# Preparing the shared weights of a mixed shared and expert layer: 5 tiles ahead and 23 in the first group

## The reference

```
x = x + (einsum('bsd,bdh->bsh', x, W[cat_ids]) + b[cat_ids][:, None, :])
h = gelu(einsum('bnd,hd->bnh', x, fc1_w) + fc1_b, approximate=False)      # 2048 hidden
shared   = einsum('bnh,sh->bns', h, fc2_w) + fc2_b                        # 384 columns
expert_x = einsum('bnh,bph->bnp', h, experts_w[indices]) + be[:, None, :] # 128 columns
x = x + concatenate([shared, expert_x], axis=-1)
```

## Time and profile before

| | |
|---|---|
| timed runs | 1692.08 us (1691.57 to 1693.65, n = 3) |
| profiled execution | 1690.38 us, of it span 1688.6 us |
| TensorE matmul | 1662.6 us busy, 98% of the span, 7297 instructions |
| VectorE | 1155.4 us, 68% |
| ScalarE | 549.1 us, 33% |
| GpSimd | 210.7 us, 12% |
| 16 DMA engines | 56.5% of their span for SyncE's queue (211.35 MB), 0.1% for ScalarE's (0.79 MB) |
| granted TensorE clock | 0.995 over the span |

### The profile page before, as it was taken

One profiled execution on the slowest core, in us unless ns is written; L12 is line 12 of the kernel. 1 busy time (PEld: TensorE's weight loads), 2 busy tenths in 40 slices (PEclk: granted clock), 3 DMA queues, 4 the chain that ended last, 5 costly groups with the idle time before them and its releaser, 6 DMA issues.

```text
span 1688.6 us, 27858 instructions
## 1 busy us (share of the span) xinstructions
PE 1662.6 (98%) x7297; PEld 1346.1 (80%) x7297; DVE 1155.4 (68%) x1944; ACT 549.1 (33%) x927; POOL 210.7 (12%) x198
## 2 busy tenths in 40 slices
PE   6799999999999999999999999999999999999999
PEld 5688888888888888888888888888888888888887
DVE  6567767676676766867666676766767667676654
ACT  5233333233233333333333333333333333332321
POOL 1020200111020110200202011110200202001010
PEclk9899999999999999999999999999999999999999
DMA  8656656556565565556555565565655656565430
GB/s 264 149 145 131 154 106 158 112 132 128 107 154 113 132 129 102 140 120 136 121 130 124 109 156 109 133 130 106 148 117 128 129 104 143 116 140 119 96 51 25
DMA packets 750033, 212.99 MB, mean 126 GB/s; under 512 B 676068, under 2 KB 690548, under 8 KB 749940
## 3 DMA queue, kind: packets, MB, share of 16 engines
q1 hardware_dynamic: 749508, 211.35, 56.5%
q10 hardware_dynamic: 432, 0.79, 0.1%
HBM read 195.24 MB, written 16.78 MB: 126 GB/s over the span
## 4 chain that ended last, share of the span: by engine, by line
PE 97%; SPq 1%; DMA 1%; issue 0%; DVE 0%; ACT 0%; DVEq 0%; ACTq 0%
PE ps_out L717 42%; PE ps_h L702 21%; PE ps_e L702 21%; PE ps_y L689 10%; PE ps_t L643 1%; PE ps_e L643 1%; SPq L320 1%; DMA w_raw<-in_L_cond_W 1%; DMA prep_raw<-in_L_cond_fc_w 0%; PE ps_out L643 0%; SPq L291 0%; DVE w_split L512 0%; SPq L327 0%; DVE resid L580 0%; SPq L302 0%
## 5 line engine op out<-in xcount | busy, mean ns | idle before, releaser
L717 PE MATMUL ps_out<-w2e,h 128*128 128x512 f32 x3072 | 761.8, 396 | 0.0
L717 PEld LDWEIGHTS ps_out<-w2e,h 128*128 128x128 f32 x3072 | 573.7, 188 | 134.7
L702 PE MATMUL ps_e<-y_t,w 128*128 128x512 f32 x1536 | 380.0, 398 | 1.4 <-DVE y_t L512 1.4
L702 PE MATMUL ps_h<-y_t,w 128*128 128x512 f32 x1536 | 379.7, 398 | 0.0
L702 PEld LDWEIGHTS ps_e<-y_t,w 128*128 128x128 f32 x1536 | 290.9, 189 | 69.8 <-DVE y_t L512 1.6
L702 PEld LDWEIGHTS ps_h<-y_t,w 128*128 128x128 f32 x1536 | 291.2, 190 | 68.1 <-DVE w L512 0.2
L568 DVE CAST h<-g_raw 128x512 fp32r<-128x512 f32 x256 | 112.2, 438 | 286.1 <-ACT g_raw L464 285.9
L452 ACT CAST w2e<-e_whole 128x512 fp32r<-128x512 f32 x256 | 158.6, 620 | 281.8 <-PE ps_out L717 272.8
L403 POOL TENSOR_TENSOR x_raw<-x_raw,b_all 128x512 f32<-128x512 f32 x60 | 82.1, 1368 | 1300.0 <-DMA x_raw<-in_x 1300.0
L689 PE MATMUL ps_y<-w_split,x_t 128*128 128x512 f32 x744 | 214.6, 396 | 2.3 <-DVE w_split L512 2.3
L512 DVE TENSOR_TENSOR w2e<-e_whole,w2e 128x512 fp32r<-128x512 f32 x256 | 198.4, 775 | 18.8 <-ACT w2e L452 13.1
(11 more groups left out here) (51 smaller groups left out, 429.1 us busy)
## 6 DMA issues: line engine op xcount, KB each, us to landing
w_raw<-in_L_cond_W SPq DMA_DIRECT2D x256, 256.0 KB, 2.9
e_blocks<-in_L_cond_experts_w SPq DMA_DIRECT2D x1024, 64.0 KB, 2.5
b_all<-in_L_cond_b SPq DMA_DIRECT2D x64, 256.0 KB, 3.5
out<-resid SPq DMA_DIRECT2D x64, 256.0 KB, 2.9
x_blocks<-in_x SPq DMA_DIRECT2D x240, 64.0 KB, 2.4
x_raw<-in_x SPq DMA_DIRECT2D x60, 256.0 KB, 3.0
prep_raw<-in_L_cond_fc_w SPq DMA_DIRECT2D x22, 256.0 KB, 3.8
be_all<-in_L_cond_experts_b SPq DMA_DIRECT2D x64, 64.0 KB, 3.1
```

The costliest lines, as they stand in the source:

```text
L702: last = nc.tensor.matmul(h_bank(c)[:, :], w1[:, w, k, c * P:(c + 1) * P], y_t[:, a, k, :, :].rearrange("p b s -> p (b s)"), start=(k == 0 ...
L717: last = nc.tensor.matmul(ps_out[b][:, :], h[:, c % 2, a, b * S:(b + 1) * S], fc2_columns(c, c % 2, w, b), start=(c == 0 and n == 0), stop ...
```

## The change

`PREP_FIRST` becomes 5: tiles 0 to 2 stand at slice 0 as before, tile 3 at slice 6 and tile 4 at slice 10. The other 23 stand in steps 0 to 11 of group 0, two a step (`PREP_RATE` = 2; step 11 has one): on TensorE the first behind fc1, the second behind the fc2 slices of chunk c - 1. Both use the bank `ps_t`. ScalarE issues every load, right behind the high half of the tile that had the slot before (`prep_later`). `PREP` is put in another order so that each tile stands before its use: two fc1 tiles, three of fc2, then four of fc1 and three of fc2 in turn, two of fc1 last.

```diff
-        PREP = ([("fc1", m) for m in range(4)] + fc2_tiles(0) + [("fc1", m) for m in range(4, 8)] + fc2_tiles(1)
-                + [("fc1", m) for m in range(8, 11)] + fc2_tiles(2) + [("fc1", m) for m in range(11, 14)]
+        PREP = ([("fc1", m) for m in range(2)] + fc2_tiles(0) + [("fc1", m) for m in range(2, 6)] + fc2_tiles(1)
+                + [("fc1", m) for m in range(6, 10)] + fc2_tiles(2) + [("fc1", m) for m in range(10, 14)]
                 + fc2_tiles(3) + [("fc1", m) for m in range(14, NC)])
-        PREP_FIRST = NPREP // 2 - 1
+        PREP_FIRST = 5
+        PREP_RATE = 2
...
-            return range(PSLOTS) if j == 0 else range(j + PSLOTS - 1, min(j + PSLOTS, PREP_FIRST))
+            return range(PSLOTS) if j == 0 else [t for t in range(PSLOTS, PREP_FIRST) if j == 2 + KD * (t - PSLOTS + 1)]
...
-            return PREP_FIRST + c if first(g) and 0 <= c < NPREP - PREP_FIRST else None
+            t = PREP_FIRST + PREP_RATE * c + n
+            return t if first(g) and t < NPREP else None
...
+        def prep_later(u):
+
+            return [t for t in range(PSLOTS, NPREP) if max(prep_earlier(t)) == u]
...
                 load_l0(0, j // KD, j % KD)
-                for t in prep_beside(j):
-                    if t >= PSLOTS:
-                        load_prep(sp, t)
...
-                    load_prep(sp, prep_in_step(g, c))
...
                 nc.scalar.copy(prep_dst(t, 0), four(prep_bank(t))).then_inc(prep_hi, 1)
+                for u in prep_later(t):
+                    load_prep(act, u)
...
                     gelu(g, c)
-                    prep_high(prep_in_step(g, c))
+                    for n in range(PREP_RATE):
+                        prep_high(prep_in_step(g, c, n))
...
                     h_high(g, c)
-                    prep_low(prep_in_step(g, c))
+                    prep_low(prep_in_step(g, c, 0))
                     if more and c % KD == KD - 1:
                         y_sum(g + 1, c // KD)
                     h_low(g, c)
+                    prep_low(prep_in_step(g, c, 1))
...
                     fc1(g, c)
-                    turn_prep(prep_in_step(g, c))
+                    turn_prep(prep_in_step(g, c, 0))
...
                         if c >= 1:
                             fc2(g, c - 1)
+                        turn_prep(prep_in_step(g, c, 1))
                         if more:
                             l0_slice(g + 1, c)
```

More of the change, by code:

```diff
@@ L162, in fc2_tiles, with prep_in_step @@
             return [("fc2", NS - 1, q)] + [("fc2", n, q) for n in range(NS - 1)]
-        PREP = ([("fc1", m) for m in range(4)] + fc2_tiles(0) + [("fc1", m) for m in range(4, 8)] + fc2_tiles(1)
-                + [("fc1", m) for m in range(8, 11)] + fc2_tiles(2) + [("fc1", m) for m in range(11, 14)]
+        PREP = ([("fc1", m) for m in range(2)] + fc2_tiles(0) + [("fc1", m) for m in range(2, 6)] + fc2_tiles(1)
+                + [("fc1", m) for m in range(6, 10)] + fc2_tiles(2) + [("fc1", m) for m in range(10, 14)]
                 + fc2_tiles(3) + [("fc1", m) for m in range(14, NC)])
-        PREP_FIRST = NPREP // 2 - 1
-        assert len(PREP) == NPREP and NPREP - PREP_FIRST <= NC
+        PREP_FIRST = 5
+        PREP_RATE = 2
+        assert len(PREP) == NPREP and NPREP - PREP_FIRST <= PREP_RATE * NC
         def prep_beside(j):
-            return range(PSLOTS) if j == 0 else range(j + PSLOTS - 1, min(j + PSLOTS, PREP_FIRST))
-        def prep_in_step(g, c):
-            return PREP_FIRST + c if first(g) and 0 <= c < NPREP - PREP_FIRST else None
+            return range(PSLOTS) if j == 0 else [t for t in range(PSLOTS, PREP_FIRST) if j == 2 + KD * (t - PSLOTS + 1)]
+        def prep_in_step(g, c, n):
+            t = PREP_FIRST + PREP_RATE * c + n
+            return t if first(g) and t < NPREP else None
         def prep_count(*tile):
```

## The result

The changed kernel takes 1694.68 us (1692.84 to 1697.62, 20 runs); the kernel before took 1691.61 us in the 20 runs beside it. The ratio is 1.0020, 95% interval [1.0013, 1.0026]: 3 us slower. I had forecast 1690.6 us, 1.5 less than before. The range held the time, the sign was wrong.

What follows compares the result with a forecast made beforehand. The prediction took TensorE's waits in the first 57 us, in the prologue and step 0, as the bound. Terms -5.0 + 0.5 + 2.5 + 0.5 = -1.5 us on 1692.08 gave 1690.6 us, range 1685.5 to 1696.5.

Steps and rivals of the forecast that it cites:

- The prologue (-5.0 us): Layer 0 slices before the first fc1: eight tiles leave, so this stretch was to get 5.0 us shorter.
- The faster rival: Prologue: slices could go at 1.2 us each, gaining 8.8 instead of 5.0 us, total 1686.8 us; chance 15%.
- The experts' chain: End of the prologue: the first expert transfers were to start 5.0 us earlier, near 30.9 instead of 35.90 us.
- Step 0, +0.5: Step 0 of group 0: TensorE's idle stays, its cause passing from a tile transfer to the expert transfers; 0.5 us slower.
- The rival with the transfer as the only wait: Step 0: only tile 13's transfer holds TensorE, so its 9.88 us go; about 1680 us; chance 4%.
- The turns, +2.5: Group 0's steps behind step 0: seven further tile turns on full TensorE at 0.35 us each, 2.5 us slower.
- The new wait, +0.5: Steps 1 to 10: second turn waits for the first tile's low half, 0.5 us for an early step or two.
- the new wait bites: Steps 1 to 10: first tile's low half late in most steps; at 1.0 us a step 1700 us; chance 13%.
- ScalarE's loads stand behind SyncE's: Steps 0 to 10: each ScalarE load waits for one expert transfer, 0.76 us; 5 us in all, 1695.6; chance 5%.

Runs made afterwards that it cites:

- b0_early: Changed kernel with group 0's four bias rows b0 put in free space of e_blocks, so SyncE does not wait for GpSimd's add: 1692.29 us, ratio 1.0007.
- before_act_loads: Kernel before, its tile order and 13 + 15 split kept, with ScalarE issuing every load behind the slot's previous high half: 1692.20 us, ratio 1.0012.
- tiles_late: Changed kernel with tiles 3 and 4 turned at slices 12 and 13 instead of 6 and 10: 1695.23 us, ratio 1.0023.
- warm: Changed kernel with extra unused identity transposes on TensorE in front of layer 0 slices 7 to 11: 1694.75 us, ratio 1.0018.
- no_adds: Changed kernel with GpSimd's adds for batch 0 cut to one column, the rest of these sums left out: ratio 1.0012.
- experts_split: Changed kernel with ScalarE issuing 8 of the first 16 expert transfers beside SyncE's 8: 1691.62 us, ratio 1.0008.

## Why the prediction was wrong

1. **The prologue (-5.0 us) is the step that failed**: the first fc1 is 1.8 us later in the trace, and from the first slice to there it is 0.7 longer. "SyncE ... its other waits are on the same slices" overlooked the wait for GpSimd's add. Its chain (sum of batch 0, add, b0 of batch 2, W slice 9 behind it) does not run through the tiles: b0 of batch 2 was issued at 20.06 before and at 20.59 after. I read the rate of 1.49 us off slices 11 to 15, where that chain had no more say; b0_early shows the rate for slices 4 to 12 once it is cut. Twelve slices at that rate are 17.9 us, and the changed kernel took 24.2. Of the 6.3 more, 4.2 stand in slices 4 to 12, where the add's chain is, and 2.1 in the first four. Two more parts: loads on ScalarE's queue come later (2.5 us with 13 tiles, before_act_loads), and behind the wait come a burst of transfers and a low clock (tiles_late, warm; in the traces 1 us each, in timed runs not to be told). The first four slices are no faster either (8.1 us after, 8.2 before; 9.2 in b0_early). ScalarE waits for their W transfers (4.6 us in all from 8 to 18 us, 3.5 before). Tiles 3 and 4 are loaded ahead of W slice 3 in both kernels, so the change takes no tile load out of its way. That transfers hold these four slices is read from the trace; no run shows it by itself. The faster rival, slices at 1.2 us each, fell with the rest.

2. **The experts' chain** moved with the prologue as I said, the wrong way (35.90 to 37.65). From the first expert issue to fc1 of step 1 it is 21.2 us before and 21.6 after.

3. **Step 0, +0.5**: right in mechanism and size. The idle stayed and moved to in front of the second turn; VectorE's low half of tile 5, 56.29 to 56.97, releases it. The distance from issue to fc1 of step 1 grew by 0.4. The idle itself is 11.3 us where I expected 9 to 10, as fc1 in front of it ran 3.03 instead of 4.57 us. The rival with the transfer as the only wait fell in before_act_loads, where 8 us of idle stay; 3.1 us of step 0 were the transfer's.

4. **The turns, +2.5**: from step 2's fc1 to group 1's the distance grew by 4.2 us, 2.4 without step 2's idle, and step 1 has one more turn of 0.39: 2.8. A step with a second turn is 0.38 to 0.45 us longer (7.13 us against 6.71 in the mean of steps 3 to 9) where I took 0.35, which is right for the turn itself (0.35 to 0.39 from its start to the next).

5. **The new wait, +0.5**: 1.76, in step 2 alone. I named VectorE's lateness there but put it down to the W slice alone; no_adds shows that the idle goes with GpSimd's adds. In the other nine steps the wait costs nothing. The rival "the new wait bites" is right in place and wrong in extent. That ScalarE's loads stand behind SyncE's did not happen: its 21 loads in the steps took 0.33 to 0.57 us each to issue, also where SyncE issued an expert transfer at the same moment (0.33 us at 80.08, beside SyncE's from 80.07). By the rule of one sequencer at a time at the descriptor block (the Trainium skill, "Perfetto Trace Analysis", "DMA Instruction — HWDGE (DVE, Sync)") one of two such issues would have to wait for the other. Little of that shows: in experts_split SyncE's eight expert issues took 5.98 us beside ScalarE's, and eight took 5.95 without them in the changed kernel (from 52.13), while ScalarE's eight took 6.78.

With +1.8 in place of -5.0, and 1.8 in place of 0.5 for the wait, the steps give +1.8 + 0.4 + 2.8 + 1.8 = 6.8, less 0.8 for fc1 of step 1, which ran 3.90 instead of 4.68 us, and less 0.6 by which the gap shrinks in group 1 (no edit reaches there): 5.4 of the 5.7 us by which the two profiled executions differ. The timed difference of 3 us is smaller, as the changed kernel's profiled execution was 1.4 us above its median and that of the kernel before 1.2 below its own. Of the forecast -1.5 us the prologue's term alone was 6.8 us off (-5.0 against +1.8); the other terms were together 1.5 us too low, 1.3 of it in the wait of step 2.

## What to carry to other kernels

Removing work from a stage gives its time back only if no other chain runs through the stage at the same pace. Suppose the engine that looks full were free, and follow the queue that issues the loads: what does the transfer in front of the one you need wait for? A rate read at the end of a stage holds only for that part of it. Where two long waits of the same length stand in a list, on two engines, look for the issue that both stand behind, and move it forward: this is what made the kernel faster here, and not the removal of the wait that was named.

## What the runs showed of the hardware

A load on ScalarE's queue is issued while the cast in front of it runs, and costs ScalarE little (changed kernel, start, time to issue):

```profile
83.31 0.59 ACT L461 CAST w<-ps_t 128x512 fp32r<-128x512 f32 x1 [2.51 <-PE ps_t L649]
83.32 0.33 ACTq L275 DMA_DIRECT2D prep_raw<-in_L_cond_fc_w  x1
83.80 0.62 ACT L439 CAST w_split<-w_raw 128x512 fp32r<-128x512 f32 x1
```

The next cast starts 0.49 us behind the last; in the kernel before it is 0.46 with no load between them (75.79 to 76.25). I had counted 0.44 us each. Eight issues in a row do block ScalarE (7.5 us in experts_split). And two operations of VectorE ran 1.53 and 1.50 instead of 0.42 and 0.69 us beside GpSimd's adds.
